# Second operands of two one-element VectorE steps in a fused perceiver kernel: read as tensors, or as per-partition scalars

## What is computed

```
x = x + _L0_xattn_ref(_layernorm(x, axis=-1), ctx_768, ...)   # 8 heads of 64, 2048 keys
x = x + _L0_attn_ref(_layernorm(x, axis=-1), ...)
x = x + _L0_ffn_ref(_layernorm(x, axis=-1), ...)

# in _L0_xattn_ref
sim  = jnp.einsum('bihd,bjhd->bhij', q, k) * SCALE
attn = jax.nn.softmax(sim, axis=-1)
out  = jnp.einsum('bhij,bjhd->bihd', attn, v)
```

## Time and profile before

| | us |
|---|---|
| median of 3 runs | 948.62 |
| lowest and highest | 947.88, 949.03 |
| the profiled execution, its own time | 949.72 |
| its span, first to last instruction | 947.7 |

### The profile page before, as it was taken

How to read it: one execution, slowest core, us unless ns; L and a number is a source line. 1 busy time by engine, 2 the same in 40 slices (tenths; PEclk the granted TensorE clock), 3 DMA queues, 4 the chain that set the end, 5 groups by cost and what they waited for, 6 DMA issues and landing times.

```text
span 947.7 us, 19492 instructions
## 1 busy us (share of the span) xinstructions
PE 908.3 (96%) x7470; PEld 566.4 (60%) x7470; DVE 600.1 (63%) x973; ACT 575.4 (61%) x1014; POOL 506.7 (53%) x393
## 2 busy tenths in 40 slices
PE   6999999999999999999999999988999899999998
PEld 4556666666666666666666666655666455544444
DVE  6645665566556656665665566566866668886634
ACT  4856676666766776666677666756666522336540
POOL 4646466456545755675466556766876766310000
PEclk9999999999999999999999999999999999999999
DMA  9366566656656576565666656866798663133502
GB/s 332 89 153 149 123 136 140 154 130 134 145 123 129 129 146 132 122 138 133 123 140 154 142 123 151 186 122 129 158 183 177 113 105 96 39 107 78 178 12 79
DMA packets 340268, 126.35 MB, mean 133 GB/s; under 512 B 316113, under 2 KB 317905, under 8 KB 340177
## 3 DMA queue, kind: packets, MB, share of 16 engines
q1 hardware_dynamic: 324832, 95.87, 48.8%
q10 hardware_dynamic: 15344, 29.23, 10.3%
HBM read 45.36 MB, written 2.10 MB: 50 GB/s over the span
## 4 chain that ended last, share of the span: by engine, by line
PE 86%; DVE 6%; ACT 4%; issue 1%; DMA 1%; SPq 1%; POOL 0%; ACTq 0%; DVEq 0%
PE v_ps L670 26%; PE k_ps L670 24%; PE e_ps L739 9%; PE e_ps L670 8%; PE o_ps L759 5%; PE e_ps L1021 3%; PE o_ps L761 3%; DVE new_max L1542 2%; PE o_ps L776 2%; DVE q_max L1537 2%; PE o_ps L1014 1%; ACT p_h L1195 1%; PE e_ps L1014 1%; DVE v L1523 1%; ACT v L1158 1%
## 5 line engine op out<-in xcount | busy, mean ns | idle before, releaser
L1979 POOL TENSOR_TENSOR p_l<-p_f,p_h 128x1024 f16<-128x1024 f32 x128 | 273.0, 2133 | 260.7 <-ACT p_f L1202 259.9
L1537 DVE TENSOR_REDUCE q_max<-e_ps 128x1 f32<-128x1024 f32 x128 | 153.4, 1219 | 49.6 <-PE e_ps L739 49.6
L1530 DVE TENSOR_TENSOR k_l<-k_ps,k_h 128x512 f16<-128x512 f32 x128 | 88.5, 692 | 125.4 <-ACT k_h L1166 125.4
L670 PE MATMUL v_ps<-wv_h,ctx_h 128*128 128x256 f16 x756 | 124.7, 274 | 24.3 <-DVE v L1523 24.3
L1195 ACT ACTIVATE p_h<-e_ps,bias 128x1024 f16<-128x1024 f32 x128 | 143.2, 1119 | 2.4 <-issue 0.3
L1523 DVE TENSOR_TENSOR v<-v_ps,v 128x512 f16<-128x512 f32 x127 | 87.6, 690 | 88.6 <-ACT v L1158 87.9
L1202 ACT ACTIVATE p_f<-e_ps,bias 128x1024 f32<-128x1024 f32 x128 | 142.0, 1109 | 0.0
L670 PE MATMUL v_ps<-wv_l,ctx_h 128*128 128x256 f16 x756 | 124.2, 273 | 0.0
L670 PE MATMUL v_ps<-wv_h,ctx_l 128*128 128x256 f16 x756 | 124.1, 273 | 0.0
L759 PE MATMUL o_ps<-v,pt_h 128*128 128x128 f16 x1024 | 104.2, 220 | 0.6 <-DVE acc L1554 0.6
L670 PE MATMUL k_ps<-ctx_h,wk_h 128*128 128x512 f16 x384 | 104.4, 381 | 0.0
(11 more groups left out here) (311 smaller groups left out, 1336.9 us busy)
## 6 DMA issues: line engine op xcount, KB each, us to landing
raw<-in_ctx_t ACTq DMA_DIRECT2D x27, 768.0 KB, 5.4
w_raw<-in_w_t SPq DMA_DIRECT2D x32, 256.0 KB, 4.0
raw<-in_ctx_t SPq DMA_DIRECT2D x4, 768.0 KB, 7.3
pt_h<-p_h SPq DMA_TRANSPOSE x128, 2.9
pt_l<-p_l SPq DMA_TRANSPOSE x128, 2.8
out<-xr SPq DMA_DIRECT2D x7, 256.0 KB, 2.0
x_in<-in_x SPq DMA_DIRECT2D x6, 256.0 KB, 8.5
o_all<-in_x ACTq DMA_DIRECT2D x6, 256.0 KB, 3.7
```

The lines of the kernel that those rows point to most:

```text
L670: mm = pe.matmul(acc, a(c), m(c), start=(i == 0), stop=(i == len(todo) - 1))
L1530: dve.tensor_tensor(k_l[:, s // 2 % K_RING, cols], k_ps[:, :], k_h[:, s // 2 % K_RING, cols], ALU.subtract)\
L1537: ins = dve.tensor_reduce(q_max[:, col:col + 1], e_ps[s % 2][:, :, :].rearrange("p i n -> p (i n)"), AX, ALU.max, negate=True)
L1979: pool.tensor_tensor(p_l[:, s % L_RING, :, :], p_f[:, s % F_RING, :, :], p_h[:, s % H_RING, :, :], ALU.subtract).then_inc(p_split, 1)
```

## The change

Both steps keep their place, their waits and their results. In `slot_maximum` the minimum of two [128, 1] columns was a `tensor_tensor` with two tensor inputs; it becomes a `tensor_scalar` with one tensor input and the old maximum as a scalar per partition. In `add_sums` the `scalar_tensor_tensor` had two tensor inputs (`p_sum` old and new) and one scalar per partition (`fade`); it becomes a `tensor_scalar` with one tensor input and two scalars per partition. There are 64 instructions of each, one per slot behind. No other instruction of any engine is added, removed or moved.

```diff
@@ slot_maximum
-                    ins = dve.tensor_tensor(new_max[:, col:col + 1], q_max[:, col:col + 1], q_max[:, old:old + 1], ALU.min)
+                    ins = dve.tensor_scalar(new_max[:, col:col + 1], q_max[:, col:col + 1], q_max[:, old:old + 1], None, ALU.min)
@@ add_sums
-                dve.scalar_tensor_tensor(o_den[:, p, h, :], p_sum[:, old:old + 1], fade[:, col:col + 1], p_sum[:, col:col + 1],
-                                         ALU.mult, ALU.add).then_inc(o_rec_ready, 1)
+                dve.tensor_scalar(o_den[:, p, h, :], p_sum[:, old:old + 1], fade[:, col:col + 1], p_sum[:, col:col + 1],
+                                  ALU.mult, ALU.add).then_inc(o_rec_ready, 1)
```

## The result

| | before, us | changed, us |
|---|---|---|
| median (4 runs each) | 948.25 | 923.55 |
| lowest and highest | 947.32, 949.03 | 922.91, 924.51 |
| profiled execution, its time and span | 949.72, 947.7 | 923.73, 921.7 |

The profiled execution of the kernel before is not among its four runs. The ratio is 0.9741, 95% interval [0.9724, 0.9758]: 2.6% faster. The forecast was 922.0 with a range of 919.5 to 929.

A forecast was written before the change was run, and what follows sets the result against it. TensorE was taken as the bound, idling where GpSimd holds VectorE's minimum. 949.72 - 26.85 (19.2 + 7.65) + 0.12 + 0.1 = 923.1, less 1.10 to the median: 922.0 us; own range 919.5 to 925, 8-in-10 range 919.5 to 929.

The forecast's parts named there:

- The bound and the cause: Batches 0 to 5: GpSimd's subtraction holds the two-tensor minimum and TensorE waits; 6 x 3.20 = 19.2 us to gain.
- the rivals: Three alternatives: minimum still held (13 in 100), scalar holds VectorE longer (7 in 100), batch 6 stays long (7 in 100).
- One element escapes: At the minimum: a one-element tensor_scalar is not held by GpSimd; gain 26.85 us if so, nothing otherwise.
- The price of a scalar: On VectorE: 0.06 us for one scalar, the minimum from 0.16 to 0.22 us; the denominator 0.28 with two.
- Its cover: Ahead of v_low in units behind: slack of 0.31 us hides 0.12 for two minima, so worth 0.
- slow start: After a TensorE wait: the 18 matmuls that follow take 2.12 instead of 1.97 us, 0.15 more.
- rival 2: Units behind: the scalar holds VectorE longer than 0.06 us; 9.9 us back, 931.9; 7 in 100.
- The denominator at nothing: The 64 denominators: freeing VectorE of some 40 us is off the path, worth 0; +0.1 us in the tail.
- Batch 6: Batch 6: falls from 93.09 to 85.44 us as waits and the clock drop go; all 7.65 us gained.
- rival 3: Batch 6 stays long: order of p_l or of transfers keeps 4.45 us, time 926.4; 7 in 100.
- The size: Whole kernel: 949.72 to 923.1 us for an execution like the profiled one, 922.0 as median, 1.10 lower.

The follow-up runs named there:

- the runs with copies: Changed kernel with the minimum of each slot behind computed twice or three times, copies to unread columns: 930.44 and 936.69 us, against 923.22 without.
- the repeated run: The changed kernel, unchanged, run again on a second chip as base for later runs: 923.22 us, ratio 0.9717 to the kernel before.

## Why the prediction was right, point by point

- **The bound and the cause.** TensorE's waits on a held minimum: right. They are gone together with the holds, and batches 1 to 6 are 85.46 us, all of it TensorE, forecast 85.4. None of the rivals is left: without the changed minimum the waits stay, with a second column they are back, and doubling GpSimd's instruction costs 45 us without the change and 6 with it.
- **One element escapes.** Right, and it decided everything: with two elements the result is 951.56. The forecast had this at 87 in 100 on an argument from the rate alone, since the nearest row, four elements, was held; no row before the run showed it. The Trainium skill's "VectorE: DVE Perf Modes", What auto-detection actually checks, asks that the outermost non-unit dimensions of source and destination be both even or equal. The prediction took this as against it (one equals one), but a single column has no non-unit dimension, so the sentence leaves the case open. "Advanced Engine Details and Errata", 2x-2p Requirements, in the Trainium skill, with its "(>1)" for an odd dimension, agrees with the runs with 1, 2 and 3 elements.
- **The price of a scalar.** Estimated 0.22 and 0.28, measured 0.214 and 0.265.
- **Its cover.** Mis-sized. The prediction put the slack ahead of `v_ps` at 0.31 us, from 461.74 + 0.15 to 462.20. The 462.20 is the time at which the chain that ended last takes up that group, not its first matmul. The timeline of TensorE in the kernel before has that one in the last row here (the first is the last matmul before the wait of the earlier trace rows):

```profile
449.83 0.19 PE L761 MATMUL o_ps<-v,pt_l 128*128 128x64 f16 x1
...
462.01 0.19 PE L761 MATMUL o_ps<-v,pt_l 128*128 128x64 f16 x1
462.04 0.49 PE L670 MATMUL v_ps<-wv_h,ctx_h 128*128 128x256 f16 x3
```

  So the slack was 0.15, the two scalars took 0.11 of it, and 0.04 are left, as the runs with copies confirm. The "slow start" of 0.15 per wait came from the same misreading (2.12 against 1.97 in the earlier trace rows), and both errors cancel: 1.65 - 0.15 = 1.50, which is what the windows said. The idle time is 1.34 and not 1.50 because the last matmul before the wait is recorded to 450.02, while without a wait the next begins 0.03 after its start, at 449.86: 0.16 of the delay is recorded as busy. That is also the 10.84 against 10.68 of TensorE's busy time in the earlier trace rows. So a wait costs 0.16 more than its idle time shows. That the prediction's sum met the 1.34 and the 1.50 was luck. Its total rested on the windows and held; rival 2 was nearer than it looked, since 0.02 us more per scalar would have cost time in 32 units.
- **The denominator at nothing.** Right for the edit alone. Not quite right in company: without it the change loses 0.75 us in batch 6, a place that the prediction did not see. At the end the forecast added 0.22 for the scalars; from the first maximum of batch 7 to the end the kernel went from 274.71 to 274.98 us, and to 274.93 in the repeated run.
- **Batch 6.** All 7.65 us went, and rival 3 with it. But about 1.6 of them were a clock drop that executions of the kernel before have in differing number. The drop near 655 is gone and the one before the tail is still there (at 719 us), as forecast.
- **The size.** By profiles the gain is 949.72 - 923.73 = 26.0, forecast 26.6. Of the missing 0.6, 0.45 lie ahead of the first maximum (39.55 against 40.00 us), where nothing was changed. By medians it is 24.7 in the first group and 26.3 where the changed kernel was run again (949.56 to 923.22). The median came out 1.55 above the forecast of 922.0, of which 0.6 are the smaller gain just given and 0.9 the step from the profiled execution to the median: the forecast took 1.10 off, and in the changed kernel the two lie 0.18 apart (923.73 and 923.55). Taking the one profiled execution for typical but for 1.1 us was good to about 1 to 2 us, no better.

## What to carry to other kernels

When a tiny VectorE instruction has a median of 0.2 us and a maximum of 3, put its end beside the ends of GpSimd's instructions: an equal end names the suspect, and doubling the GpSimd instruction, with and without the change, tries it. A [128, 1] statistic is best read as a scalar operand, with one single column as the tensor; it costs some 0.05 us more when alone, so look first at what slack stands behind it, and measure slack to the first matmul in the timeline, not to an entry of a chain. Change all short two-tensor steps of such a row together, or the next one can take over the hold, as once in batch 6 here.

## What the runs showed of the hardware that I had not expected

- A `tensor_scalar` on fp32 columns in SBUF is free of GpSimd at 1 element (214 ns, 64 of 64) and held at 2 and at 3 (up to 2.91 and 2.92 us). Two and three elements take the same 228 ns.
- GpSimd holds VectorE also when it reads one tensor; for a two-tensor minimum the hold then ended 863 to 867 ns before GpSimd's recorded end, 14 times of 14, against 13 to 18 ns after it in two-tensor subtractions. A two- or three-column `tensor_scalar` begun 365 to 376 ns before the end of a one-tensor GpSimd instruction was held to 22 or 23 ns after it, six times of six.
- TensorE's clock fell to 0.50 for 3.4 us behind some waits of 2.4 us and not behind others of the same length in the same kernel (of the first and third waits of batch 6, behind the third alone in one profile, behind both in another), which moves this kernel by 1.6 us each time.
